# One kernel, seven parts of one change: output projection with the mean folded into its weight, batch 1's queries and keys in the prologue, 16 probability buffers with products by pairs of key chunks, and a reordered end

## The reference

```python
xn = layernorm(x)                                   # no weights
q, k, v = xn @ Wq + bq, xn @ Wk + bk, xn @ Wv + bv  # 8 heads of 16
attn = softmax(q @ k.T / 4)                         # per batch and head, 512 x 512
lam = exp(sum(lq1 * lk1)) - exp(sum(lq2 * lk2)) + 0.8
o = attn @ v[head % 4] - lam * (attn @ v[4 + head % 4])
s = (0.2 * (layernorm(o) * ln_w + ln_b)) @ Wo + bo
h = mod(int(xn[:, 0] + xn[:, 1]), 8)                # expert of a token, and h + 1
y = mean of the two experts' relu(xn @ W1 + b1) @ W2 + b2
out = x + s * silu(y)
```

## Time and profile before

| | us |
|---|---|
| Median of 3 runs | 457.02 |
| The profiled execution, its own time | 457.09 |
| Its span in the trace | 455.0 |
| TensorE busy, share of the span | 406.6, 89% |
| VectorE busy | 337.2, 74% |
| ScalarE busy | 236.0, 52% |
| GpSimd busy | 127.5, 28% |

### The profile page before, as it was taken

One profiled execution on the slowest core, in us unless ns is written; L12 is line 12 of the kernel. 1 busy time (PEld: TensorE's weight loads), 2 busy tenths in 40 slices (PEclk: granted clock), 3 DMA queues, 4 the chain that ended last, 5 costly groups with the idle time before them and its releaser, 6 DMA issues.

```text
span 455.0 us, 8683 instructions
## 1 busy us (share of the span) xinstructions
PE 406.6 (89%) x2672; PEld 251.9 (55%) x2672; DVE 337.2 (74%) x936; ACT 236.0 (52%) x543; POOL 127.5 (28%) x154
## 2 busy tenths in 40 slices
PE   1917889999999999898999999999999999998683
PEld 1314666565666757575656757575666657552122
DVE  6788785767687777687677777787787876867954
ACT  4550435555645545564546554564555555556670
POOL 5701142233231411424123151243242222200101
PEclk9955999999999999999999999999999999999996
DMA  7998243232703144303604145211806430345220
GB/s 253 306 297 269 85 132 131 72 123 59 262 23 120 48 134 153 124 16 105 220 14 175 42 127 172 98 55 38 260 22 187 141 127 14 126 132 182 99 75 23
DMA packets 36805, 57.34 MB, mean 126 GB/s; under 512 B 6350, under 2 KB 24376, under 8 KB 36762
## 3 DMA queue, kind: packets, MB, share of 16 engines
q1 hardware_dynamic: 28937, 49.19, 32.0%
q0 software_dynamic: 2496, 5.12, 4.3%
q10 hardware_dynamic: 5328, 2.49, 2.0%
HBM read 14.02 MB, written 6.75 MB: 46 GB/s over the span
## 4 chain that ended last, share of the span: by engine, by line
PE 71%; DVE 12%; issue 5%; ACT 5%; DMA 4%; POOL 1%; ACTq 0%; POOLq 0%; DVEq 0%
PE ring L1180 13%; PE pv_bank L1125 12%; PE score L1084 12%; PE ring L1195 12%; PE exp L1113 10%; DVE neg_max L842 4%; PE ring L1050 3%; DMA xs<-xn_rows,inverse 2%; PE ring L1149 2%; PE ring L1171 2%; PE ring L1133 1%; ACT xn L625 1%; PE ring L1073 1%; DVE stats_o L889 1%; DMA xn_rows<-xn 1%
## 5 line engine op out<-in xcount | busy, mean ns | idle before, releaser
L650 ACT ACTIVATE probs<-exp 128x512 f32<-128x512 f32 x244 | 141.6, 600 | 121.8 <-PE exp L1113 118.5
L842 DVE TENSOR_REDUCE neg_max<-score 128x1 f32<-128x512 f32 x256 | 172.2, 685 | 30.3 <-PE score L1084 19.9
L1084 PE MATMUL score<-ks,qs 96*128 96x512 bf16 x256 | 98.9, 390 | 10.8 <-DVE neg_max L842 10.1
L1113 PE MATMUL exp<-qs,ks 99*128 99x512 bf16 x244 | 92.1, 381 | 3.3 <-ACT probs L650 1.4
L584 POOL DMA_INDIRECT y_rows<-y_sb,y_row x39 | 39.7, 1018 | 188.8 <-DVE y_sb L974 188.4
L1180 PEld LDWEIGHTS ring<-xsT,pair 128*128 128x128 f32 x624 | 80.3, 193 | 15.4 <-issue 10.2
L1180 PE MATMUL ring<-xsT,pair 128*128 128x128 f32 x624 | 84.7, 279 | 0.6 <-issue 0.6
L1195 PEld LDWEIGHTS ring<-w_sb,hT 128*128 128x128 f32 x624 | 74.6, 192 | 5.9 <-issue 1.7
L1195 PE MATMUL ring<-w_sb,hT 128*128 x624 | 77.6, 277 | 0.0
L672 ACT ACTIVATE hT<-ring,pair 128x128 f32<-128x128 f32 x172 | 49.2, 370 | 45.6 <-PE ring L1180 43.8
L1125 PE MATMUL pv_bank<-probs,va 128*32 128x512 f32 x512 | 68.2, 605 | 0.8 <-ACT probs L650 0.7
(11 more groups left out here) (150 smaller groups left out, 345.7 us busy)
## 6 DMA issues: line engine op xcount, KB each, us to landing
pair<-table SPq DMA_DIRECT2D x39, 580.0 KB
qs<-parts SPq DMA_DIRECT2D x48, 128.0 KB
...
```

Source lines behind the costliest of these rows:

```text
L650: a.activation(probs[:, n % PR, :], exp_banks[n][:, :], ACT.Exp, scale=SCALE).then_inc(exp_done, 1)
L842: v.tensor_reduce(neg_max[:, b % 2, col:col + 1], score_bank[n % 2][:, :], AX.X, ALU.max, negate=True).then_inc(max_taken, 1)
L1084: t.matmul(score_bank[n % 2][:, :], qs[0:MAX_ROW, b % STK, hh, c * P:(c + 1) * P], ks[0:MAX_ROW, b % STK, hh, :], start=True, stop=True).t ...
L1113: t.matmul(exp_banks[n][:, :], ks[0:KROWS, b % STK, hh, kc * P:(kc + 1) * P], qs[0:KROWS, b % STK, hh, :], start=True, stop=True).then_inc ...
```

## The change

What it does, in seven parts:

1. **Centred projection.** The mean of o is no longer subtracted from o. `turn_z` transposes `attn` itself, and `wo_eff` has its column means subtracted (one more matmul of ones with `wo_eff` in `bias_o`), which gives the same product. `rstd` is multiplied in where the product is read: four instructions on 128x128 (`scalar_tensor_tensor`) in place of one on 128x512. `scale_o` and the tile z are gone.
2. **Batch 1 in the prologue.** `PEELED` is (0, 1). Its six partial projections run on PE and ACT before `invert`; their parts lie in buffers of `probs`, and the 12 DMAs that stack them are issued at positions 12.1 to 12.6, behind a wait for the first expert tile's result.
3. **16 probability buffers** (eight of them in the tile that held x), **and pv by two key chunks**: one step of 8 matmuls after every 8 exponentials, except for the last two groups (`PV_TAIL`).
4. **Biases first.** The expert biases are loaded on ACT's queue, spread by PE before anything else into the banks of scores and exp, and copied by ACT in one step (`bias_copy`) instead of two on ACT and two on DVE.
5. **Prologue order.** W2 loads are dealt over ACT's order one to three at a time, POOL normalises four batches instead of two, SP issues the small loads ahead of six stores of `xn`, the tables of the first 3 expert tiles are made ahead of the others, `rows` is cut 10, 10, 8, 4 instead of four times 8.
6. **Expert tiles every 6.2 positions** instead of 6.0, so that the last one's result is at 247 and not at 240. `load_y` moves from 242.6 to 249.
7. **End.** `split_max` comes ahead of `norm_o`, `turn_z` and `project_o` come earlier, `finish` steps move by up to 2.2 positions later. y is read into `qs` and `ks`.

The core of the diff:

```diff
-PR = 8
+PR = 16
+PV_GROUPS = 2
+PV_TAIL = 2
-POOL_NORM = (6, 7)
+POOL_NORM = (4, 5, 6, 7)
-PEELED = (0,)
+PEELED = (0, 1)
-FFN_PACE = 6.0
+FFN_PACE = 6.2
-Z_SLACK = 4
+NORM_O, TURN_Z, PROJECT_O = 42.6, 41.5, 45.5
-LOAD_Y_AT = 242.6
+LOAD_Y_AT = 249
-ROW_GROUPS = 4
+ROW_ENDS = (10, 20, 28, 32)
...
-            if n % 4 == 3:
-                at(n + LAG + PV_OFF, "pv", n // 4)
+            if n % 4 == 3 and n // 4 >= PV_STEPS - PV_TAIL:
+                at(n + LAG + PV_OFF, "pv", n // 4, 1)
+            elif n % (4 * PV_GROUPS) == 4 * PV_GROUPS - 1:
+                at(n + LAG + PV_OFF, "pv", n // 4 - PV_GROUPS + 1, PV_GROUPS)
...
+                    first, groups = s[1:]
+                    pe.wait_ge(exp_done, 4 * (first + groups))
+                    for n4 in range(first, first + groups):
...
                 elif kind == "stack_part":
                     b, i, k = s[1:]
                     sp.wait_ge((high_ready, mid_ready, low_ready)[k], 2 * b + i + 1)
+                    if b == 1:
+                        sp.wait_ge(y_ready, 1)
...
-                    pe.wait_ge(z_ready, b + half + 1)
+                    pe.wait_ge(attn_ready, 2 * b + 2)
                     free(uses[s])
                     for i in range(n):
-                        last = t.transpose(shared[:, i * P:(i + 1) * P], z[:, c + i, :], ident[:, :])
+                        last = t.transpose(shared[:, i * P:(i + 1) * P], attn[:, b % 2, c + i, :], ident[:, :])
...
-                    v.tensor_tensor(s_sb[:, C * b:C * b + C, :], shared[:, :].rearrange("p (c n) -> p c n", c=C),
-                                    bo_eff[:, :].unsqueeze(1).to_broadcast([P, C, D]), ALU.add).then_inc(s_ready, 1)
+                    dve.wait_ge(rstd_o_ready, b + 1)
+                    for c in range(C):
+                        last = v.scalar_tensor_tensor(s_sb[:, C * b + c, :], shared[:, c * D:(c + 1) * D],
+                                                      rstd_o[:, c:c + 1], bo_eff[:, :], ALU.mult, ALU.add)
+                    last.then_inc(s_ready, 1)
```

270 lines of the change are left out of this document (145 added, 125 removed).

## The result

The changed kernel takes 454.9 us (median of 9 runs, 453.12 to 456.27) against 457.38 for the kernel before (9 runs, 456.12 to 460.72): ratio 0.994, interval 0.9914 to 0.9965. I forecast 444.4 and a range of 439.5 to 451.0. The sign was right; the time is 10.5 us above the forecast, and of the gain of 12.7 us 2.5 came. The profiled execution took 454.33 us, with a span of 452.6 (before: 457.09 and 455.0).

What follows compares the result with a forecast made beforehand. PE bounds the main part, the way to the first expert tile the prologue, a chain of waits the end. Terms 0.5 + 2.5 + 2.8 + 0 + 1.5 + 2.8 + 2.6 = 12.7 off 457.09 give 444.4 us, range 439.5 to 451.

Steps and rivals of the forecast that it cites:

- First expert tile: Prologue: shorter DVE path to `inverse` lets the first tile's gather go at about 37.8 to 38.1, 0.5 us earlier.
- (a): SP's prologue queue: small loads ahead of six `xn` stores; stores issued by 32.1, the last landing at 37.8 us.
- Rival A: Prologue: bias matmuls and batch chains queued on PE make the first tile 3 us late; 447.9 us, chance 0.15.
- (b): Prologue, PE and ACT: batch 1's twelve matmuls ahead of `invert` fit PE's free 12 us; chain ends by about 34.
- Batch 1: First expert tiles: moving batch 1's projection into the prologue saves 2.5 us, ends 1.4 and 3.7.
- Rival D: Prologue: PE's work on batch 1 ends the half clock before the first tile, 2 us; total 441.2, chance 0.13.
- Pairs: pv steps: pairing 62 of 64 saves 31 entries of 0.09 us, 2.8 us; ends 0 and 6.2.
- Rival C: pv steps: the second group exposes its weight load like the first, so pairs save nothing; 447.2 us, chance 0.12.
- Rival B: pv steps: pairs starve DVE and ACT, slower from 0.41 us a pair; 459.9 us at 0.5, chance 0.05.
- Stretched expert work: Towards the end: expert tiles up to position 247 fill PE's idle time, saving 1.5 us; ends 0.5 and 2.6.
- Last score to last product: End: waits for z and for the last maxima's DMA go, saving 2.8 us; ends 1 and 4.
- Tail: Behind the last product's start: z, transpose, copy and projection run beside statistics and power, saving 2.6 us; lower end 2.0.

Runs made afterwards that it cites:

- e2: Changed kernel with the last w1 block and ten small loads issued behind the last six stores of `xn`: median 2.2 us lower.
- e18: e13 with batch 1's projection moved out of the prologue, back among the first expert tiles: slower by 4.3 us by the ratios, 5.9 by the medians.
- e7: Changed kernel with stores first, last root off GpSimd, and load 2 gated: waiting for the first tile's result, ahead of the stacking transfers: 449.13 us.
- e1: Changed kernel with single probability products instead of pairs, sixteen buffers kept: ratio 0.9972, median 1.8 us higher.
- e13: Changed kernel with stores first, load 2 gated, last root off GpSimd, transposes 2.3 positions ahead, last eight products single: 445.51 us, ratio 0.9747.
- e15: e7 with transposes 2.3 positions ahead and all products single: ratio 0.9758, median 0.6 us from that of e13.
- e12: e7 with the tail edit, the last eight probability products single instead of the last two: 448.75 us, ratio 0.9791.
- e17: e13 with expert tiles every 6.0 positions, transposes 1.5 positions ahead, and the reload of x kept at its position: 447.03 us, ratio 0.9747.
- e10: e7 with each expert tile's transpose 2.3 positions ahead of its first weights instead of 1.5: 446.55 us, ratio 0.9743.
- e16: Kernel before the change, with each expert tile's transpose 2.3 positions ahead of its first weights instead of 1.5: 10.8 us slower.

## Why the prediction was wrong

The sum failed in four of its terms, and nearly all of the miss was in the order of the instructions, not in what the change computes. By stages of the two traces: up to score 32 I had 3.0 us and 0.5 came; from there to score 255, 4.3 (pairs and stretch) and 0.2 came; from score 255 to the last product, 2.8 and 1.45; behind it, 2.6 and 0.3. By the terms:

- **First expert tile, forecast 0.5 us early, measured 2.5 late at its transpose: the step that failed is (a).** I moved the small loads at the 7.1 us that they took before, and priced a store at the 0.5 us of one row (L450). On their new place the small loads were issued until 30.85 instead of 29.1, the six stores until 35.9 instead of 32.1, and the gather waited for them until 41.67. Cost against the same kernel with the stores first: 3.3 us at score 255. Rival A had this size (3 us) and "the gather for stores" among its signs, at 0.15, but what it argued from was TensorE's queue. (b) nearly held: `invert` began at 34.9 us, not by 34, and that delayed `inverse` by 1.0 us (37.43 and 36.45 in e2), which lay hidden behind the stores. What makes an issue long stays open. The longest (1.54 and 1.93 us) stand beside ScalarE's W2 issues (1.64 and 2.73), but the last two stores (1.17 and 1.55) come after ScalarE's last issue. The Trainium skill ("DMA: Bandwidth & Descriptors", Issuing engines are not separate DMA queues), which I cited for the shared 16 DMA engines, has the transfers interleave; the trace agrees (0.74 busy from 24 to 48 us), but the rule gives no figure for an issue.
- **Batch 1, forecast 2.5:** in the changed kernel the way from the first transpose to score 32 is 3.0 us shorter (35.5 and 38.5), near the term, and the late first tile hid it: the gain at score 32 was 0.5 us. With the tile in time it was worth 4.8 at score 32 (e18), since hardly any of batch 1's work on TensorE had been free. Rival D's cause, the clock, failed: from 40 to 48 us it is 0.50 to 0.53 in the changed kernel, as before. The "free" stacking transfers made TensorE wait 1.1 us for load 2; without that wait nothing was won in the end (e7).
- **Pairs, forecast 2.8:** TensorE is relieved of 6.9 us, and 2.3 us of it reach the end by the profiles, 1.8 by the medians (e1), and 0.6 in e13's kernel (e15). The size is about right by luck: entry and spacing both shrink (from its start to the next matmul a pair takes 1.85 us, two singles take 1.98 and an entry of 0.09 more), and waits take two thirds back. Rival C is refuted: the second group starts 0.88 us behind the first (in each of the 31 pairs), not 0.99. The Trainium skill's rule behind it ("TensorE: Matmul & The Clock Gate", The mechanism) doesn't decide here: the same section lets a weight load be pulled ahead also when it goes to the background weight buffer, which I had left out. Rival B was right in kind: 6.9 less 2.3 is 0.15 us of new waits a pair, against the 0.41 from which it decides.
- **Centred projection in the main part, forecast 0:** nothing on TensorE is seen to wait for it. No run takes this part out, so its worth is not measured.
- **Stretched expert work, forecast 1.5: wrong in sign where the transposes stand.** I filled the end's idle time and took the main part's shortening as free. With 6.2 each tile falls on another fraction of a position; at some of them four short matmuls lie between the transpose and the weights, and TensorE waits for a copy that stands behind other work of VectorE: 3.4 us in 10 waits. e12 against e17: 1.1 us lost in the traces, 1.7 in the medians, not clear of their spread. Early transposes (e10) give 2.6 us.
- **Last score to last product, forecast 2.8:** 1.45. The wait for z went and the one for the maxima fell from 1.4 to 0.6 us, and with single products the stretch is 2.95 us shorter than before (19.65 to 16.7, e1 and e12); the pairs that I put into it gave 1.5 back by starving ScalarE, which I had written down as that term's lower end.
- **Tail, forecast 2.6:** 2.6 on the path and 0.3 at the end, because GpSimd's drain of 7.54 us starts at the power. In the kernel before it ended at 454.4 us and the outputs at 454.6, a tie that I didn't see since I read the tail up to the last product and not up to the end of the span.

Four edits undid these losses in e13: stores (2.2 to 3.4 us), drain (2.2), transposes (2.6), products in the end (0 to 1.3). They make 7 to 9.5 us; e13 is 9.4 us below the changed kernel by the medians and 8.8 by the ratios. Open are some 0.8 us of the stretch from score 32 to 255 (4.1 missing; the stretch of tiles makes 2.6 of it and the pairs 0.7, since those 223 scores take 343.2 us in e1 and 341.1 in the changed kernel), how the 10.8 us of e16 divide, and the exact worth of gate and tail. Biases first, the order of the prologue but for the stores, and the order of the end were never taken out alone.
